# Where a layer's first loads are issued from: an identity made on chip, one merged load of constants, one load from ScalarE's queue

## The reference, cut to what matters

```python
x = L0_attn_x                                  # (2, 4096, 256)
xn = _layernorm(x, axis=-1)
# branch 1: D = a fractal dimension of the first 1024 numbers of xn; a filter made of D,
#   x1 = ifft(fft(xn) * filt).real ; bits = sigmoid(x1 @ W_el + b_el) > 0.5 ; corrected bits
#   return x1 + corrected @ W_le + b_le
# branch 2:
h = gelu(einsum('bse,eh->bsh', xn, w1) + b1)   # 256 -> 1024, exact gelu
ffn = einsum('bsh,he->bse', h, w2) + b2        # 1024 -> 256
x = x + branch1 + ffn
```

## Time and profile before

| | before |
|---|---|
| median of 3 runs | 408.74 us (408.49 to 408.76) |
| the profiled execution's own time | 408.33 us |
| its span | 406.5 us |
| PE busy | 401.1 us, 99% of the span |
| DVE / ACT / POOL busy | 73% / 55% / 22% |
| chain that ended last | PE 97%, DVE 1%, DMA 1% |
| DMA | 35.75 MB, mean 88 GB/s |

### The profile page before, as it was taken

How to read it: one execution, slowest core, us unless ns; L and a number is a source line. 1 busy time by engine, 2 the same in 40 slices (tenths; PEclk the granted TensorE clock), 3 DMA queues, 4 the chain that set the end, 5 groups by cost and what they waited for, 6 DMA issues and landing times.

```text
span 406.5 us, 5533 instructions
## 1 busy us (share of the span) xinstructions
PE 401.1 (99%) x1768; PEld 328.7 (81%) x1768; DVE 298.1 (73%) x511; ACT 223.3 (55%) x333; POOL 88.2 (22%) x102
## 2 busy tenths in 40 slices
PE   8999999999999999999999999999999999999996
PEld 4888888888888888888888888888888888888885
DVE  6889975878668795677957688486874879657654
ACT  3966646457354764537545464555636556364551
POOL 3153411313003131121313013131121313013000
PEclk9999999999999999999999999999999999999999
DMA  7544333213333213232123333023333121111011
GB/s 203 200 157 156 103 105 104 67 40 102 105 104 103 58 46 104 103 103 104 53 54 100 103 104 102 29 75 103 104 103 102 49 56 52 52 52 52 2 52 52
DMA packets 15307, 35.75 MB, mean 88 GB/s; under 512 B 5440, under 2 KB 6592, under 8 KB 15296
## 3 DMA queue, kind: packets, MB, share of 16 engines
q1 hardware_dynamic: 15152, 35.49, 26.5%
q10 hardware_dynamic: 144, 0.13, 0.1%
HBM read 27.17 MB, written 8.45 MB: 88 GB/s over the span
## 4 chain that ended last, share of the span: by engine, by line
PE 97%; DVE 1%; DMA 1%; POOL 0%; SPq 0%; issue 0%; DVEq 0%
PE p_h L955 43%; PE p_f L973 28%; PE p_f L978 14%; PE p_s L1012 5%; PE p_l L999 4%; PE p_s L1020 2%; DMA x_sb<-x 1%; DVE xt_sb L790 0%; SPq L246 0%; DVE stats L821 0%; POOL row_nums L359 0%; DVE rows_sb L808 0%; PE p_f L988 0%; DVE xT_lo L830 0%; DVE w_lo L795 0%
## 5 line engine op out<-in xcount | busy, mean ns | idle before, releaser
L444 ACT ACTIVATE h<-p_h,small_sb 128x512 f32<-128x512 f32 x128 | 88.2, 689 | 141.6 <-PE p_h L955 141.3
L631 DVE TENSOR_TENSOR h_lo<-h,h_hi 128x512 fp32r<-128x512 f32 x128 | 103.0, 804 | 71.2 <-ACT h_hi L452 71.2
L973 PE MATMUL p_f<-h_hi,w_hi 128*128 128x512 f32 x254 | 99.3, 391 | 0.0
L973 PE MATMUL p_f<-h_hi,w_lo 128*128 128x512 f32 x254 | 98.9, 389 | 0.0
L367 POOL TENSOR_TENSOR uv<-xn 128x512 f32<-128x512 f32 x30 | 59.3, 1998 | 125.9 <-DVE xn L616 125.9
L452 ACT CAST h_hi<-h 128x512 fp32r<-128x512 f32 x128 | 79.5, 621 | 5.8
L955 PE MATMUL p_h<-xT_hi,w_hi 128*128 128x512 f32 (+1 forms) x258 | 79.4, 389 | 0.0
L955 PE MATMUL p_h<-xT_lo,w_hi 128*128 128x512 f32 (+1 forms) x258 | 79.2, 388 | 0.1
L955 PE MATMUL p_h<-xT_hi,w_lo 128*128 128x512 f32 (+1 forms) x258 | 79.3, 389 | 0.0
L978 PE MATMUL p_f<-h_lo,w_hi 128*128 128x512 f32 x254 | 78.2, 389 | 0.0
L955 PEld LDWEIGHTS p_h<-xT_lo,w_hi 128*128 128x128 f32 x258 | 48.3, 188 | 10.6 <-DVE xT_lo L830 0.3
(11 more groups left out here) (112 smaller groups left out, 319.8 us busy)
## 6 DMA issues: line engine op xcount, KB each, us to landing
xt_sb<-xt SPq DMA_DIRECT2D x16, 512.0 KB, 5.3
x_sb<-x SPq DMA_DIRECT2D x15, 512.0 KB, 4.7
rows_sb<-rows_dram SPq DMA_DIRECT2D x15, 512.0 KB, 4.3
out<-xt_sb SPq DMA_DIRECT2D x15, 512.0 KB, 2.9
xt_sb<-w SPq DMA_DIRECT2D x3, 512.0 KB, 7.2
xt_sb<-w SPq DMA_DIRECT2D x2, 256.0 KB, 4.2
x_sb<-x SPq DMA_DIRECT2D x2, 128.0 KB, 2.1
x_sb<-x SPq DMA_DIRECT2D x1, 256.0 KB, 3.0
```

Of the source, the lines that this page charges most:

```text
L444: nc.scalar.activation(h[m % 2][:], p_h[:, m % 2, :], ACT.Gelu, bias=small_sb[:, S_B1 + m:S_B1 + m + 1]).then_inc(gelu_done, 1)
L631: nc.vector.tensor_tensor(h_lo[m % HR][:], h[m % 2][:], h_hi[m % HR][:].bitcast(F32), ALU.subtract).then_inc(h_lo_done, 1)
L973: mm(p_f[:, a, :], w[:, m, a * HF:(a + 1) * HF], h_hi[r][:], start=(m == 0 and w is w2_hi), stop=False, skip_group_check=True)
```

## The change

The identity is no longer loaded: GpSimd makes it with one affine select from `ones`, after a wait for its own three memsets and before the memsets of `cw` and `le2`. The tables `con` become the tail of `small_sb`, one input and one load of 197 columns (98.5 KB) instead of two of 60 and 137; it is issued behind the second part of w1. Tile 1 of chunk 0 is issued from ACT's queue, as the first thing of ACT's block.

```diff
-        small_sb = sb("small_sb", [P, S_END], F32)
+        small_sb = sb("small_sb", [P, S_END + K_END], F32)
...
-        con = sb("con", [P, K_END], F32)
+        con = small_sb[:, S_END:S_END + K_END]
...
@@ block.sync
-            for cols, arrived in ((slice(0, E), x_first[0]), (slice(E, HALF * E), x_first[1]),
-                                  (slice(HALF * E, CW), x_in[0])):
+            for cols, arrived in ((slice(0, E), x_first[0]), (slice(HALF * E, CW), x_in[0])):
                 sp.dma_start(x0[:, cols], x_rows[:, cols]).then_inc(arrived, 16)
...
-            sp.dma_start(id_sb[:], ident).then_inc(id_in, 16)
             load_w1(0)
+            load_w1(1)
             sp.dma_start(small_sb[:], small).then_inc(small_in, 16)
-            load_w1(1)
-            sp.dma_start(con[:], consts).then_inc(con_in, 16)
             load_w2(0)
...
@@ block.gpsimd
             nc.gpsimd.memset(ones[:], 1.0).then_inc(pool_set, 1)
+            pool.wait_ge(pool_set, 3)
+
+            nc.gpsimd.affine_select(out=id_sb[:], in_=ones[:], pattern=[[1, P]], base=0, channel_multiplier=-1,
+                                    compare_op=ALU.is_equal, fill=0.0).then_inc(id_made, 1)
             for q in range(2):
                 nc.gpsimd.memset(cw[q][:].bitcast(F32), 0.0).then_inc(cw_set, 1)
                 nc.gpsimd.memset(le2[q][:].bitcast(F32), 0.0).then_inc(le_set, 1)
-            pool.wait_ge(pool_set, 3)
...
@@ block.scalar
+            second = slice(E, HALF * E)
+            act.dma_start(x_sb[0][:, :, :].rearrange("p j e -> p (j e)")[:, second],
+                          x_rows[:, second]).then_inc(x_first[1], 16)
             act.wait_ge(pool_set, 2)
             nc.scalar.activation(early[:], eps[:], ACT.Gelu)
...
@@ block.vector
-            dve.wait_ge(con_in, 16)
+            dve.wait_ge(small_in, 16)
...
@@ block.tensor
-            pe.wait_ge(id_in, 16)
+            pe.wait_ge(id_made, 1)
```

More of the change, by code:

```diff
@@ L62, with build @@
 S_END = S_WEL + KB * LAT
-def build(nc, x, xt, small, latent, w1, w2, ident, consts, basis, out):
+def build(nc, x, xt, small, latent, w1, w2, basis, out):
     ctx = ExitStack()
@@ L174, in build @@
         w2_in = [sem(f"w2_in{i}") for i in range(len(W2_LOADS))]
-        id_in, con_in, basis_in, small_in = sem("id_in"), sem("con_in"), sem("basis_in"), sem("small_in")
+        id_made, basis_in, small_in = sem("id_made"), sem("basis_in"), sem("small_in")
         latent_in, stored = sem("latent_in"), sem("stored")
@@ L1202, in constants @@
     assert a.sum(axis=1).min() >= 4
-    return np.eye(P, dtype=f4), con, basis
+    return con, basis
 def layouts(inputs):
@@ L1217, in layouts @@
     small = np.concatenate([on_rows(inputs["L0_ffn_b1"], MB), on_rows(inputs["L0_attn_b_le"], KB),
-                            on_rows(inputs["L0_ffn_b2"], KB), on_rows(inputs["L0_attn_W_el"], KB)], axis=1)
+                            on_rows(inputs["L0_ffn_b2"], KB), on_rows(inputs["L0_attn_W_el"], KB),
+                            constants()[0]], axis=1)
     latent = np.concatenate([np.asarray(inputs["L0_attn_b_el"])[:, None], np.asarray(inputs["L0_attn_W_le"])], axis=1)
@@ L1238 @@
     arrays = {name: np.ascontiguousarray(a) for name, a in layouts(inputs).items()}
-    for name, a in zip(("ident", "consts", "basis"), constants()):
+    for name, a in zip(("basis",), constants()[1:]):
         arrays[name] = a
```

## The result

| | before | after |
|---|---|---|
| median | 408.57 us (8 runs, 408.47 to 409.09) | 410.14 us (8 runs, 409.55 to 411.08) |
| ratio after / before, 95% interval | | 1.0037 (1.0028 to 1.0046) |
| profiled execution, own time | 408.33 us | 410.09 us |
| its span | 406.5 us | 408.4 us |

The kernel became slower by 1.57 us, where 0.40 less was forecast. The time lies outside the range.

What follows compares the result with a forecast made beforehand. PE was taken as the bound from 8.87 us, leaving only the head, bound by chunk 0's third piece (tiles 2 and 3). Terms -0.40 + 0 + 0 + 0 = -0.40 took the median from 408.74 to 408.34 us; range 408.0 to 409.0.

Steps and rivals of the forecast that it cites:

- the part on the merged load: Load of small_sb and tables at the fifth queue place: first readers past 10 us, so cost 0.
- From 8.87 on all work is released by PE or by landed loads, so it moves forward as a block.: After the head: any gain before 8.87 us carries unchanged to the end, with no further term.
- PE is busy for 391.13 us of 391.13: From 8.87 to 400 us: PE waits for nothing, so no earlier load shortens this stretch.
- The margin of w1's third part: Load issued at 5.44, landing at 12.64 for a cast at 13.35: margin 0.7, growing with three queue places gained.
- Tile 1 on ACT's queue, -0.40: Head: one SP issue less puts the third piece up to 0.46 us earlier; taken as 0.40 gained.
- Does tile 1 itself come late?: Start of the head: tile 1 on ACT's queue lands at 3.04, 0.28 before it is needed; no cost.
- sign of error: Prediction wrong if POOL's first inverse root comes after 4.7, L815 starts after 3.2, or PE gaps after 9 us.
- the first rival: Head: two queues share DMA engines, tile 0 lands up to 0.39 later, gain only 0.1 to 0.2; chance 0.28.
- The identity from GpSimd, 0: POOL before the first inverse root: select of 0.50 and library under 1.5 fit the 2.19 us gap; cost 0.
- POOL becomes late: Rival: library plus select exceed POOL's gap, first inverse root slips, loss up to 0.8, 409.5 us; chance 0.14.
- The signs: Start times in us expected in the after profile's head for the third piece, DVE, POOL, PE and w1's cast.
- the three rivals: Gain doesn't arrive (408.5 to 408.8, chance 0.28); POOL late (0.14); more than issue time gained (408.2, 0.03).

Runs made afterwards that it cites:

- Experiment 1: The changed kernel with 32 unused bytes behind the identity's tile, so tiles from bias on lie where they lay before: 408.24 us against 408.66 of the kernel before.
- experiment 2: The kernel before with 32 unused bytes ahead of bias, no load or instruction changed: 409.86 us against 408.66 of the kernel before.
- experiment 5: The kernel before with 64 unused bytes ahead of cor, so cor and le2 start at multiples of 128 bytes: 407.81 us against 408.72.
- experiment 6: The kernel before with 64 unused bytes ahead of bias, moving all tiles from bias on: 409.71 us against 408.72.
- experiment 7: The kernel before with only cw, the latents' weights, moved by 32 bytes: 409.25 us against 408.72.
- experiment 11: The kernel before with 64 unused bytes behind cor, so only le2 is newly aligned: 408.54 us against 408.61.
- experiment 10: The whole change with 32 unused bytes behind the identity and 64 ahead of cor, all TensorE operands at multiples of 128 bytes: 407.31 us, ratio 0.9967.
- experiment 3: The kernel before with only tile 1 of chunk 0 issued first on ACT's queue, SBUF places unchanged: 408.11 us against 408.66.

## Why the prediction was wrong

**The step that failed** is the part on the merged load, "this is hidden by a wide margin either way", costed at 0 in the sum, and with it the sentence that closes it, "From 8.87 on all work is released by PE or by landed loads, so it moves forward as a block." I costed the load, its place in the queue and its readers. I didn't cost the line `con = small_sb[...]`, which moves every later tile by 32 bytes. It costs 0.107 us a chunk, 1.67 us in the profile, a term that the sum doesn't have. Experiment 1 takes it away with nothing else changed, and experiment 2 makes it in the old kernel. "PE is busy for 391.13 us of 391.13" is true and was read for too much: a busy PE has no waits, but its matmuls can be longer. The busy share is blind to that. In the kernel after, the stretch from 10 to 400 us still shows PE busy for 389.88 of 390.00, with 1717 matmuls in it, where the kernel before has 1726:

```profile
10.00:400.00 390.00, 389.88 (x1717) 320.65 (x1716) 287.89 (x488) 218.30 (x325) 83.88 (x87) 1.00 0.27 84
```

**The margin of w1's third part** ("a margin of 0.7, and with three places gained in the queue ... it grows") was wrong as well: issued 1.38 earlier, it landed at 13.7, where before it had landed at 12.6, and the cast waited 0.51 for it. Two things failed. The margin of 0.7 was that of one lucky execution: the same queue has the load there at 13.2 to 13.6 in the profiles of experiments 2, 5, 6, 7 and 11. And the earlier issue didn't make this load earlier. The DMA engines are full from 10 to 14 us in both kernels; by stretches of 2 us, the kernel before (PEclk, DMA share and GB/s at the row's end), then the kernel after:

```profile
10.00:12.00 2.00, 2.00 (x11) 1.68 (x11) 1.03 (x5) 1.63 (x3) 0.00 (x0) 1.00 1.02 418
12.00:14.00 2.00, 2.00 (x12) 1.67 (x11) 1.77 (x7) 1.97 (x5) 0.00 (x0) 1.00 1.07 408
```

```profile
10.00:12.00 2.00, 2.00 (x11) 1.63 (x10) 1.18 (x5) 1.83 (x4) 0.00 (x0) 1.00 1.02 411
12.00:14.00 2.00, 2.00 (x12) 1.67 (x10) 1.56 (x6) 1.46 (x3) 0.00 (x0) 1.00 1.01 382
```

The loads of 512 KB land one after the other there, 1.3 us apart: at 11.3, 12.6 and 13.9 before, at 12.4, 13.7 and 15.0 after. 512 KB in 1.3 us is about 400 GB/s, the rate of the rows. So when a load of this row lands is set by the bytes ahead of it, which the change lowers by 64 KB alone, and by what the engines lost before 10 us, and that differs from execution to execution: with the queue of after the third part landed at 13.7, 13.2 (experiment 1) and 12.0 (experiment 10).

**Tile 1 on ACT's queue, -0.40**: the size held on the whole (-0.55 alone, -0.42 for the change with the tiles' places restored), the path didn't. "Does tile 1 itself come late?" was answered with no. It does: L815's successor starts at 3.51, past the 3.2 that I named as a sign of error. The time of a piece on ACT's queue, 2.3 us, came from a store at the end of the program, issued at 403.56 while SP's queue issued two more from 403.21 on the earlier trace rows, and not from loads at the start. (The prediction's "No row of before has both queues at work" overlooks this one.) With both queues at work at the start the first two tiles need 2.7 and 2.9 us:

```profile
x_sb<-x SPq DMA_DIRECT2D x1, 128.0 KB, 2.7
x_sb<-x ACTq DMA_DIRECT2D x1, 128.0 KB, 2.9
```

That is the mechanism of the first rival, and larger than its 0.39. It reached the first inverse root with 0.44 (4.63 for 4.19), and since POOL comes to the second only at 5.61, behind the first, the second pair gained 0.14 to 0.20 of its 0.46. The Trainium skill ("DMA: Bandwidth & Descriptors", section "Issuing engines are not separate DMA queues") says that loads of several issuing engines share the same 16 and save only issue time; by that rule tile 0 gets later, and the trace agrees (landing 2.7 us after its issue, not 2.1). That the size held is in part luck: 0.20 of the 0.40 is in the head of the two profiles, and the rest of the medians' difference is that the profile of before is a fast execution (experiment 3).

**The identity from GpSimd, 0**: right. The select took 0.29 us, not 0.50, and started as soon as `ones` was set; the memsets ended at 2.44, 2.2 us before the first inverse root. The library instruction left no visible time. With the identity on GpSimd all issues start 0.05 later; from which of its instructions this comes isn't shown. The Trainium skill ("GPSIMD Engine Reference", section "Instruction dispatch") gives about 6 us for a first call to freshly loaded routines; no such time is in this trace, and the rival "POOL becomes late" is refuted. Whether the instruction loads anything here isn't shown.

**The signs.** "Third piece issued at 1.18": 1.23. "L821 near 4.2": 4.46. "First inverse root stays at 4.19": 4.63. "Second near 5.3": 5.61. "Cast of w1 before 6.4": 6.45. "Transposes of pair 0 at 6.35 to 6.45": 6.56. "Transposes of pair 1 at about 7.25": 7.47. "PE without a stop from 8.45": from 8.67, with a new wait at 18.8, which I had named as a sign of error. Of the three rivals none had the mechanism that decided: the one on the slower side looked for a late engine, not for slower work.

## What to carry to other kernels

A declaration is an edit too: when a tile is added, dropped, merged or resized, work out where the tiles behind it land, and keep the operands of such matmuls at multiples of 128 bytes. Only fp32r matmuls, and places 0, 32, 64 and 96 off, were looked at here. If the total time moves and no wait explains it, compare the start of the same matmul in both traces: a step points to a wait, a slope to work that has become slower, even where the busy share says 99% in both. A load's landing time belongs to the queue and to the execution in which it was measured: look at several profiles before a margin of 0.7 us carries a zero.

## What was not expected of the hardware

- fp32r matmuls of 128x512 whose weights or moving operand lie 32, 64 or 96 bytes off a multiple of 128 mostly take 390 to 398 ns instead of 389, and the spacing goes from 0.224 to 0.228 us up to 0.229 to 0.237. Some matmuls just behind them, and in the kernel after the one just ahead too, are slow with aligned operands: 24 spacings a chunk in the kernel after, where the latents, the filter and `le_products` are 12 matmuls. Why the effect outlasts the operand is open. The Trainium skill ("SBUF — State Buffer", section "Operand start alignment") asks only for a multiple of the element's size and says that this is about legality, with nothing timed; the runs show that for TensorE the place has a price as well.
- 64 bytes that nobody uses, ahead of `cor`, are worth more than the whole change: 0.9 us against 0.4.
- Two queues at once at the start make the first 128 KB land 0.6 us later than one (2.7 for 2.1), and the kernel still becomes faster (experiment 3).
- With the same queue and the same issue times, a 512 KB load at 4.06 us lands at 12.0 to 13.7 in three executions; behind a full row of loads the earlier issue bought nothing.
